# Conditioned residual block: weights stationary and results feature-major, with norm factors fetched by matmul

## The reference

```python
h = _ln(_ln(x, pw_g[pathway], pw_b[pathway]), cp_g[kind], cp_b[kind])
t = _ln(x, tm_g[kind], tm_b[kind]);  s = _ln(x, ms_g[scale], ms_b[scale])
m, n, r = (x + _mlp_ln(state) for state in (memory, noise, resource))   # state of the batch
cat = concat([w[0]*h, w[1]*t, w[2]*m, w[3]*n, w[4]*r, w[5]*s]);  w = softmax(aw)
x1 = x + _ln(silu(cat @ int_W1 + int_b1) @ int_W2 + int_b2, int_g, int_be)
styles = w256 @ (affine_w / 16).T + affine_b;  dcoefs = rsqrt(sum((weight*styles)**2) + 1e-8)
out = x1 + clip((x1 * styles) @ weight.T * dcoefs + bias, -256, 256)
```

## Time and profile before

| | us |
|---|---|
| median of 3 runs | 1377.66 (1376.0 to 1379.78) |
| the profiled execution | 1377.71 |
| its span, first to last instruction | 1375.9 |
| TensorE busy | 1302.4 |
| VectorE busy | 950.1 |
| GpSimd busy | 854.6 |
| ScalarE busy | 271.1 |

### The profile page before, as it was taken

How to read it: one execution, slowest core, us unless ns; L and a number is a source line. 1 busy time by engine, 2 the same in 40 slices (tenths; PEclk the granted TensorE clock), 3 DMA queues, 4 the chain that set the end, 5 groups by cost and what they waited for, 6 DMA issues and landing times.

```text
span 1375.9 us, 19128 instructions
## 1 busy us (share of the span) xinstructions
PE 1302.4 (95%) x6068; PEld 1015.7 (74%) x6068; DVE 950.1 (69%) x1654; ACT 271.1 (20%) x463; POOL 854.6 (62%) x896
## 2 busy tenths in 40 slices
PE   6898999999999999999999999999999999999997
PEld 1267777777777777777777777777777777777875
DVE  1878677677677767667766776776777677676674
ACT  1321111212211221121121112112112211211210
POOL 0265666766766666676666666667666666666751
PEclk9999999999999999999999999999999999999999
DMA  9823333332333333333343333424334333332410
GB/s 297 279 71 111 110 106 113 115 110 87 125 116 102 109 108 111 109 119 107 90 137 108 100 104 111 128 88 125 101 100 127 108 107 97 121 119 87 126 54 24
DMA packets 87952, 156.99 MB, mean 114 GB/s; under 512 B 7184, under 2 KB 46480, under 8 KB 87776
## 3 DMA queue, kind: packets, MB, share of 16 engines
q0 software_dynamic: 18432, 83.89, 19.7%
q1 hardware_dynamic: 69504, 72.90, 16.9%
HBM read 139.96 MB, written 16.81 MB: 114 GB/s over the span
## 4 chain that ended last, share of the span: by engine, by line
POOL 53%; issue 35%; DVE 7%; PE 2%; POOLq 2%; DVEq 1%; DMA 0%; ACT 0%; SPq 0%
POOL work L239 7%; POOL work L390 7%; POOL work L374 7%; POOL work L388 6%; POOL work L234 6%; POOL work L397 6%; POOL work L372 3%; DVE work L741 3%; POOL rs_u L379 3%; POOL work L242 3%; DVE work L563 3%; POOL rs_x L379 2%; POOL ids_now L368 1%; POOL work L244 1%; DVE work L730 1%
## 5 line engine op out<-in xcount | busy, mean ns | idle before, releaser
L771 PEld LDWEIGHTS tb<-ident,work 128*128 128x128 f32 x1280 | 151.5, 141 | 30.4 <-DVE work L234 2.2
L771 PE MATMUL tb<-ident,work 128*128 128x128 f32 x1280 | 171.3, 273 | 2.6 <-DVE work L234 1.8
L379 POOL TENSOR_TENSOR rs_a<-ve_a,half 128x1 f32<-128x1 f32 x64 | 35.1, 548 | 210.5 <-DVE ve_a L546 210.5
L563 DVE TENSOR_SCALAR work<-xt,mv_x,rs_x 128x512 f32<-128x512 f32 x64 | 35.0, 546 | 185.0 <-POOL rs_x L379 185.0
L239 POOL TENSOR_TENSOR work<-work,norm_g 128x512 f32<-128x512 f32 x62 | 103.3, 1666 | 94.4 <-DVE work L741 94.4
L451 ACT ACTIVATE lhs_hi_t<-tb 128x512 fp32r<-128x512 f32 x64 | 38.3, 599 | 552.0 <-PE tb L771 552.0
L841 PE MATMUL py<-w_hi_l,lhs_lo_l 128*128 128x512 f32 x256 | 76.5, 421 | 43.4 <-DVE lhs_lo_l L551 43.4
L837 PE MATMUL pre<-w_hi_h,lhs_hi_h 128*128 128x512 f32 x256 | 113.6, 444 | 0.0
L730 DVE SCALAR_TENSOR_TENSOR work<-work,rs_u 128x512 f32<-128x512 f32 x64 | 48.1, 752 | 93.8 <-POOL rs_u L379 93.8
L571 DVE TENSOR_TENSOR work<-work 128x512 f32<-128x512 f32 x64 | 112.5, 1757 | 0.0
L388 POOL TENSOR_TENSOR work<-work 128x512 f32<-128x512 f32 x64 | 82.3, 1285 | 47.3 <-DVE work L563 47.3
(11 more groups left out here) (160 smaller groups left out, 3044.6 us busy)
## 6 DMA issues: line engine op xcount, KB each, us to landing
xt<-x_in SPq DMA_DIRECT2D x64, 256.0 KB, 2.7
xturn<-x_turned SPq DMA_DIRECT2D x64, 256.0 KB, 3.3
out<-work SPq DMA_DIRECT2D x64, 256.0 KB, 2.0
batch_rows<-batch_rows_dram SPq DMA_DIRECT2D x16, 256.0 KB, 3.7
sel_in<-sel_ids SPq DMA_DIRECT2D x64, 48.0 KB, 2.3
work<-int_w SPq DMA_DIRECT2D x2, 1024.0 KB, 14.3
early_hi_l<-mlp_w SPq DMA_DIRECT2D x1, 1024.0 KB, 7.8
early_hi_w<-mlp_w SPq DMA_DIRECT2D x1, 1024.0 KB, 12.5
```

What stands on the lines that cost most here:

```text
L379: nc.gpsimd.tensor_tensor(rs[n][:, u, :], ve[n][:, u, :], half[:], ALU.pow).then_inc(rstd_ready[n], 1)
L771: last = pe.transpose(tb[:, bank, c * P:(c + 1) * P], src[:, c * P:(c + 1) * P], ident[:])
```

## The change

The roles are swapped. Tokens go in 16 groups of 512. A weight block of 128x128 is stationary, 512 tokens move, and the result has features on the partitions: `pre` is now four banks (512 features x 512 tokens), `uy` two banks that w2's and l1's results use in turn, `turn` two banks for all turns and fetches. A unit is 4x4 blocks x 3 = 48 matmuls of 512 columns.

- Inputs of t, s, w2 and l1 need no turn. Only h is made with tokens on the partitions and turned (`turn_h`).
- The norm factor of a token is needed along the free dimension. The per-token rstd and -mean*rstd are spread over 96 columns (`expand_stat`, VectorE), turned (`rows_in`, PE), masked with the ids (`pick_rows`), split (`split_rows`, `low_rows`), and a matmul with the gain table (`gain`) gives gain x rstd for 128 features x 512 tokens, which VectorE multiplies with turned x (`make_t`, `make_s`). `offsets` adds the rest with `tab["b"]`.
- W2 is centred in the prologue (row means subtracted), so u has mean zero over features. Its variance is the sum of four squares (ScalarE) over chunks, added on VectorE, then summed over partitions by two matmuls with a constant 1/512 matrix (`variance`). Its inverse root is eight linked VectorE operations on 128x512 (`find_root`).
- The batch rows (MLPs) are added as a per-partition bias in the Silu; gain, offset and bias of later steps are per-partition scales and biases on ScalarE.
- GpSimd keeps the powers of the per-token variances and the gathers (pathway rows of 4 KB, three buffers; kind rows of 2 KB, one buffer); its tensor operations go.
- Loads of x and turned x, and stores, are per group and feature chunk; the output is stored feature-major and turned on the host.
- All loops are written out; no hardware loop is left. Group i's t, s, h and x share the loop body with l1 of group i-1.

The diff, cut to the new bodies (the removed ones are those printed above). The first part is VectorE's, from `fill` on it is TensorE's:

```diff
+GROUP = 512
+TPG = GROUP // P
+GROUPS = TOKENS // GROUP
...
+            def first_norm(t):
...
+                nc.vector.scalar_tensor_tensor(out=g, in0=xt_tile(t), scalar=mvx[:, t % 4, 0:1], in1=g,
+                                               op0=ALU.subtract, op1=ALU.mult).then_inc(a1_done, 1)
+                nc.vector.scalar_tensor_tensor(out=g, in0=g, scalar=stat[:, t % 4, 0:1], in1=b,
+                                               op0=ALU.mult, op1=ALU.add).then_inc(a_done, 1)
...
+                nc.vector.bn_stats(raw6[:, 1, :], g).then_inc(a_stats, 1)
+                nc.vector.bn_aggr(mva[:, t % 2, :], raw6[:, 1, :]).then_inc(a_moments, 1)
+                nc.vector.tensor_scalar(vea[:, t % 2, :], mva[:, t % 2, 1:2], EPS, None, ALU.add).then_inc(a_var, 1)
...
+            def make_x1(i, c):
+                dve.wait_ge(uy_read, 8 * i + c + 1)
+                dve.wait_ge(root_ready, i + 1)
+                nc.vector.tensor_tensor(ug[:, c, :], ug[:, c, :], root[:], ALU.mult).then_inc(xq_done, 1)
...
+                nc.vector.tensor_tensor(xT[:, i % 2, c, :], ug[:, c, :], xT[:, i % 2, c, :], ALU.add).then_inc(x1_raw, 1)
...
+            def finish(i, o):
+                dve.wait_ge(uy_read, 8 * i + C + o + 1)
+                nc.vector.tensor_scalar(ug[:, o, :], ug[:, o, :], CLAMP, -CLAMP, ALU.min, ALU.max).then_inc(clipped, 1)
+                dve.wait_ge(clipped, i * C + o + 1)
+                nc.vector.tensor_tensor(xT[:, i % 2, o, :], ug[:, o, :], xT[:, i % 2, o, :], ALU.add).then_inc(y_done, 1)
...
+            for i in range(GROUPS):
...
+                make_s(i, 2)
+                if i:
+                    add_square(i - 1, 3)
+                low_s(i, 1)
+                low_h(i, 0)
+                if i:
+                    low_sum(i - 1)
+                low_s(i, 2)
+                if i and more:
+                    x_moment(f)
+                if i:
+                    find_root(i - 1)
+                make_s(i, 3)
+                low_s(i, 3)
+                low_h(i, 1)
...
+                first_norm(f - 1)
+                low_h(i, 2)
...
+                second_norm(f - 1)
+                low_h(i, 3)
...
+                if i:
+                    all_x1(i - 1)
+                for c in range(C):
+                    low_x(i, c)
...
+                if more:
+                    x_moment(f + 1)
+                    expand_stat(f)
+                    first_norm(f)
+                if i:
+                    finish(i - 1, 0)
+                if more:
+                    second_norm(f)
+                    expand_stat(f + 1)
+                    first_norm(f + 1)
+                if i:
+                    finish(i - 1, 1)
+                if more:
+                    second_norm(f + 1)
+                    x_moment(f + 2)
+                if i:
+                    finish(i - 1, 2)
+                if more:
+                    expand_stat(f + 2)
+                    first_norm(f + 2)
+                    x_moment(f + 3)
+                if i:
+                    finish(i - 1, 3)
+                if more:
+                    second_norm(f + 2)
+                    expand_stat(f + 3)
+                    pick_rows(n)
+                low_hid(i, 0)
+                low_hid(i, 1)
+                if more:
+                    low_rows(n)
...
+            def fill(*use):
...
+                if k >= 2:
+                    pe.wait_ge(*last_read(uses[k - 2]))
+                return turn[:, k % 2, :]
...
+            def rows_in(i, js=range(TPG)):
+                for j in js:
...
+                    pe.wait_ge(e_ready, i * TPG + j + 1)
...
+            def unit_y(i, o):
...
+                for c in range(C):
+                    pe.wait_ge(x1_hi, i * C + c + 1)
+                    pe.matmul(bank, w_hi["l1"][:, c, cut], hi["a"][:, c, :], start=c == 0, stop=False)
+                    pe.matmul(bank, w_lo["l1"][:, c, cut], hi["a"][:, c, :], start=False, stop=False)
+                    pe.wait_ge(x1_lo, i * C + c + 1)
+                    last = pe.matmul(bank, w_hi["l1"][:, c, cut], lo["a"][:, c, :], start=False, stop=c == C - 1)
...
+                unit_t(i, 0)
+                gain("s", i, 2)
+                unit_t(i, 1)
+                turn_h(i, 0)
+                unit_t(i, 2)
+                if i:
+                    variance(i - 1)
+                unit_t(i, 3)
+                gain("s", i, 3)
...
+                unit_s(i, 0)
+                turn_h(i, 1)
+                unit_s(i, 1)
+                turn_h(i, 2)
+                unit_s(i, 2)
...
+                turn_h(i, 3)
+                unit_s(i, 3)
+                if i:
+                    offsets(i)
...
+                for c in range(C):
+                    unit_h(i, c)
...
+                    for o in range(C):
+                        unit_y(i - 1, o)
+                        if more:
+                            rows_in(n, (o,))
+                    for o in range(C):
+                        unit_x(i, o)
+                for o in range(C):
+                    if more:
+                        gain("t", n, o)
+                    unit_u(i, o)
+                if more:
+                    gain("s", n, 0)
+                    gain("s", n, 1)
+                if not i:
+                    demod()
```

More of the change, by code:

```diff
@@ L76, in build @@
[L76 removed]
+        k_ids = sb("k_ids", [P, TILES], I32)
         half = sb("half", [P, 1])
[L78 to L90, removed]
@@ new lines, in gain, with turn_h @@
+            def gain(which, i, c):
+                bank = fill("g" + which, i, c)
+                pe.wait_ge(rows_ready, i + 1)
+                if i == 0:
+                    pe.wait_ge(tab_ready[which], 1)
+                pe.matmul(bank, tab[which][:, c * P:(c + 1) * P], rows[:], start=True, stop=True).then_inc(turn_filled, 1)
+            def turn_h(i, j):
+                bank = fill("h", i, j)
+                t = i * TPG + j
+                pe.wait_ge(gate_done, t + 1)
+                transposes(bank, gb[:, t % GBUF, 1, :], P, P)
@@ new lines, in unit_t, with unit_s, unit_h, offsets @@
+            def unit_t(i, c):
+                by_chunk("t", i, c, "a", t_hi, i * C + c + 1, t_lo, i * C + c + 1, t_used, first=c == 0)
+            def unit_s(i, c):
+                by_chunk("s", i, c, "b", s_hi, i * C + c + 1, s_lo, i * C + c + 1, s_used)
+            def unit_h(i, c):
+                by_chunk("h", i, c, "c", h_hi, (i + 1) * TPG, h_lo, (i + 1) * TPG, h_used)
+            def offsets(i):
+                for o in range(C):
+                    last = pe.matmul(pre[:, o, :], tab["b"][:, o * P:(o + 1) * P], rows[:], start=False, stop=False)
+                last.then_inc(b_used, 1)
@@ new lines, in batch_rows @@
+            def batch_rows():
+                pe.wait_ge(cT_ready, 3)
+                for n, m, w in (("r", 2, wr_in), ("m", 0, wm_in), ("n", 1, wn_in)):
+                    pe.wait_ge(ld[f"w_{n}"], 16)
+                    for c in range(C):
+                        last = pe.matmul(uy[0:QUAD, 0, :], mhT[:, c, QUAD * m:QUAD * (m + 1)], w[:, c, :],
+                                         start=n == "r" and c == 0, stop=n == "n" and c == C - 1)
+                    last.then_inc(batch_mm[n], 1)
+                bank = fill("batch")
+                pe.wait_ge(batch_copied, 1)
+                transposes(bank, mh[0:QUAD, :], QUAD, QUAD)
@@ L763, in _, with demod @@
+            def demod():
+                bank = fill("dcoef")
+                pe.wait_ge(l1_sq, 1)
+                pe.wait_ge(style_sq, 1)
+                for o in range(C):
+                    for c in range(C):
+                        last = pe.matmul(bank[:, o * BATCH:(o + 1) * BATCH], squares[:, c, o * P:(o + 1) * P], small[:, 0, c, :],
+                                         start=c == 0, stop=c == C - 1)
+                last.then_inc(turn_filled, 1)
             pe.wait_ge(ld["ident"], 16)
-            pe.wait_ge(mlp_h, 1)
+            rows_in(0)
@@ L888 @@
+            variance(GROUPS - 1)
+            for o in range(C):
+                unit_y(GROUPS - 1, o)
 def kernel(**inputs):
```

1513 lines of the change are left out of this document (865 added, 648 removed).

## The result

| | before | after |
|---|---|---|
| median | 1378.32 | 1446.24 (1438.37 to 1448.0) |
| the profiled execution | 1377.71 | 1438.37 |
| its span | 1375.9 | 1436.6 |
| TensorE busy | 1302.4 | 1252.8 |
| VectorE busy | 950.1 | 951.2 |

The account below looks back on a forecast made before the run. TensorE was taken to set the period, now waiting on VectorE's fixed order: 145 (group 0) + 14 x 82.7 + 104.5 (last group and end) + 1.8 = 1409, say 1410 us, range 1335 to 1452.

Parts of the forecast that it names:

- group 0, up to unit_t(1, 0): Start of the kernel: t weights scaled at 19 us, TensorE work 101, waits 25; 145 us (135 to 160).
- one of 14 groups: Steady group: TensorE work 72.5 us, waits 8.7, slow clock 1.5; period 82.7 us.
- last group and end: Last u block at 72.2 us, then variance to store 30.6 and a low clock 1.7; 104.5 us.
- 0.7, 0.7, 4.2 and 3.1 us: TensorE's waits a group: two at turn_h, two at the factor rows of the next group's last two tiles; 8.7 us.
- The period without the low clock: Steady group at full clock: 72.5 us of TensorE work plus 8.7 of waits, 81.2 against 80.8 before.
- one low stretch a group: After the two factor-row waits TensorE's clock halves once a group, costing 1.5 us, within 0 to 3.2.
- dense matmuls stand around them: Around the 4.2 and 3.1 us waits: dense work makes the clock loss uncertain, 0 to 3.2 us a group; 1.5 taken.
- The sum for both waits, 1434: Clock falls to half rate at both factor-row waits: 14 x 1.7 us more, 1434 us.
- Rival D: VectorE's chain does not hold TensorE and the waits vanish: 14 x 10.2 us less, 1267; chance 0.07.
- Rival C: Matmul spacing loses its unexplained 0.020 us since tokens now move: 5.0 us a group less, 1340; chance 0.13.
- the kind rows' gather: GpSimd's gather for tile f+1, wanted at 48.1 us: between 0 and 0.6 us a group, taken as 0.
- Rival B: Clock falls at both waits and VectorE loses time beside GpSimd's powers: 1.7 + 1.0 us a group more, 1448; chance 0.18.

Follow-up runs that it names:

- the kernel with the late rows: Changed kernel with the factor-row turns of each group's last two tiles moved behind the first and third x blocks: 1296.92 us, ratio 0.942 to before.
- the gate first: On top of the kernel with the late rows, VectorE does the last tile's second normalisation and the factor rows' low parts earlier: 1294.57 us, ratio 0.939 to before.

## Why the prediction was right or wrong

The sum put beside the profiled execution of after, in its own steps (us):

| | predicted | measured |
|---|---|---|
| group 0, up to unit_t(1, 0) | 145 | 155.5 |
| one of 14 groups | 82.7 | 84.12 |
| last group and end | 104.5 | 103.5 |
| outside the span | 1.8 | 1.8 |
| sum | 1409 | 1438.4 |

**Right: the mechanism and its price.** The waits of a steady group were to be 0.7, 0.7, 4.2 and 3.1 us, and are 0.47, 0.70, 4.24 and 3.07, plus 0.24 at the row of tile f+1. (In the other groups the third is 3.96 to 4.46.) They came out of the distances between VectorE's starts, taken along its order, and not from its sum. That the 4.24 agrees so closely is partly luck: from the end of y block 0 to the turn it was to be 10.1 us and is 10.56, and TensorE, with its 0.24, comes to the turn 0.4 us later too. The period without the low clock was to be 81.2 us; with the waits filled it is 81.2. VectorE's idle time stands in the x units, as said. Rival D, that the waits vanish, had the price 1267 and isn't what happened; it is nearly what the kernel with the late rows does (1297).

**Mis-sized: the clock, 1.5 us a group.** This is the largest term of the error. The prediction took one low stretch a group, at a price of 1.5 us that no row of before gave, where the forecast's own bounds went to 3.2. The filled waits show 3.4 by the medians, 48 us in all instead of 21 + 1.7. Even that is not one number: within one execution groups with nearly the same waits take 82.2 or 85.2 us, that is a loss of about 1.1 or 4.1, and the four runs of the changed kernel differ by 10 us, where the kernel without these waits stays within 1. The profiled execution is the fastest of the four, 8 us under the median, which is why the sum above ends at 1438 and not at 1446. What failed is "dense matmuls stand around them" as a reason to halve the cost: the clock fell all the same. In the short group shown, six slow matmuls behind the first wait are all, near the 1.5 forecast; in the long one the whole block between the waits is slow, and the x block behind them for some eight matmuls. The others fit: block and second wait take 7.4 to 7.5 us in all five short groups and 8.6 in six of the seven long ones. Why a group is short or long is open. The sum for both waits, 1434, which stood beside the rule of the Trainium skill (TensorE: Matmul & The Clock Gate, section Loop structure matters more than you think), was the nearer one. Its example is a long wait between every two matmuls, which takes TensorE to half rate; the trace agrees for two waits with twelve matmuls between them: the granted clock is 0.81 in the stretch after the first wait, and 0.66 in the group before.

**Too short: group 0, by 10.5 us.** It is all in the start. The first t unit was to begin at 19 us and begins at 29.7; from there to the end of the group the prediction had 126 us and the trace has 125.8. The step that failed took the weights as the last thing to be ready, scaled at 19 us. They came late too: ScalarE could start on them only at 20.2 and had them scaled at 22.2. But the unit waited for more, as PE's timeline shows:

```profile
14.84 0.80 PE L974 MATMUL turn<-ident,expand 128*96 128x128 f32 x2 [2.13 <-DVE expand L613]
19.89 1.22 PE L985 MATMUL turn<-rows,tab_t 96*128 96x512 f32 x2 [4.24 <-DVE rows L647]
23.85 1.39 PE L985 MATMUL turn<-rows,tab_t 96*128 96x512 f32 x2 [2.74 <-DVE tmp_a L658]
27.91 0.80 PE L985 MATMUL turn<-rows,tab_s 96*128 96x512 f32 x1 [2.67 <-DVE tmp_a L658]
...
29.70 1.91 PE L1006 MATMUL pre<-hi_a,w_hi_t 128*128 128x512 f32 x4
```

The factor rows, their tables and the products with turned x come one after another through VectorE, with the first tile's normalisation and the weights' low part between them; two turn banks hold the fetches back behind these products. I had priced this chain for the steady group and not for the start. The first u block came at 136.6 instead of 128, 8.6 late of these 10.5. So what lies between agrees only as a sum: the waits at the turns of group 1's rows were 7.9 + 4.7 + 3.4 = 16.0, not 11, and others were shorter.

**A small gain given back: the spacing.** 0.2333 was kept, and it is 0.2275 in the t, s and h units and 0.2267 in the others: 302 x 0.006 = 1.8 us a group less. Rival C had asked for all of 0.020. The Trainium skill (same page, section Back-to-back issue gap) gives 216 ns for 512 columns by its formula, and 131 for a sustained stream; the trace has 227 here and 233 before, and the measurement decides. The gain isn't seen in the period, because about as much is lost around turns and waits: with the late rows a group takes 74.2 us, 2.0 of them waits, so 72.2, where 302 x 0.2271 + 2.0 makes 70.6.

**Taken as nothing: the kind rows' gather.** VectorE waits 0.33 us on it in the group shown, 8.7 us in all 14 times. 4.9 of these are two waits in group 0, and the second of them, 2.5 us, lies right ahead of the row for which TensorE waited 7.9. The other twelve make 0.3 us a group, the middle of what was given. In the group shown the wait lies in the chain of the 4.24 us: the kind row has one buffer, so the gather goes out only behind the normalisation that has read the row before, and what VectorE does meanwhile takes 0.33 us less than the gather. A shorter order of VectorE alone would gain nothing in that piece.

**Rival B** (1448) is nearest to the median by its number. Its clock half is what happened, at 3.4 us a group where B had 3.2 (1.5 of the forecast and 1.7 more). Of its other half, 1.0 us a group for VectorE beside GpSimd's powers, 0.16 us is seen: the clip of 802.18 ran beside a power and took 0.59 us, as did one in each of the 14 groups, and the other 50 clips took 0.42 or 0.43, as before.

## What to carry to other kernels

When work on the bounding engine takes its input from a hand-written order on another, walk that order operation by operation from the last thing it must wait for; the busy share said 66% while the walk gave the 4.2 and 3.1 us to a tenth. A small instruction (here a 0.3 us turn) in the middle of dense work belongs where its producer is surely done; moving two of them gave 149 us, for 0.5 us a group of new waits. A wait count over a whole run holds the start's long waits too: take those out before dividing by the groups. Count such waits on TensorE at more than their length (here 10.7 us for 7.3), since the low clock behind them is paid too, and walk the start of the kernel as carefully as its steady part.

## What the runs showed of the hardware that was not expected

- Waits of about 4.2 and 3.1 us in each group, with dense matmuls before and after, brought TensorE to 1.2 GHz for part of the group, at 3.0 to 3.4 us a group on average: about 1.1 us in five groups and 4.1 in seven, for nearly the same waits. Dummy matmuls in the waits kept it at 2.4 GHz and gave 48 us back.
- A 512-column fp32r matmul is 0.2333 us from its neighbour in the program before, in runs of 12 or 48, and 0.2267 in the x units of the changed one, whichever operand moves and in either order.
- A 128x1 power on GpSimd took 0.92 to 1.00 us beside VectorE's second normalisation (all 19 in the trace with the gate first) and 0.55 to 0.57 beside a low part (all 16 with the late rows). VectorE's 128x512 clip took 0.59 us in the 14 cases where it ran beside the power of a tile's first variance, and 0.42 or 0.43 in the 50 others.
